# Inverse roots of the rows' variances: on GpSimd by its power operation, in place of VectorE's integer guess and three Newton steps

## What is computed

```python
def _layernorm(x, axis=-1, eps=1e-05):
    m = jnp.mean(x, axis=axis, keepdims=True)
    v = jnp.var(x, axis=axis, keepdims=True)
    return (x - m) / jnp.sqrt(v + eps)
...
    x = L0_attn_x
    xn = _layernorm(x, axis=-1)
    x = x + _L0_attn_ref(xn, ...) + _L0_ffn_ref(xn, ...)
    xn = _layernorm(x, axis=-1)
    x = x + _L1_attn_ref(xn, ...) + _L1_ffn_ref(xn, ...)
```

## Time and profile before

| | |
|---|---|
| time, median of 3 runs | 1029.79 us (1029.18 to 1029.96) |
| the profiled execution's own time | 1030.44 us |
| its span, first to last instruction | 1028.6 us |
| PE busy | 987.3 us (96%) |
| DVE busy | 837.6 us (81%) |
| POOL busy | 767.6 us (75%) |
| ACT busy | 757.0 us (74%) |

### The profile page before, as it was taken

How to read it: one execution, slowest core, us unless ns; L and a number is a source line. 1 busy time by engine, 2 the same in 40 slices (tenths; PEclk the granted TensorE clock), 3 DMA queues, 4 the chain that set the end, 5 groups by cost and what they waited for, 6 DMA issues and landing times.

```text
span 1028.6 us, 23734 instructions
## 1 busy us (share of the span) xinstructions
PE 987.3 (96%) x8004; PEld 678.5 (66%) x8004; DVE 837.6 (81%) x2271; ACT 757.0 (74%) x2014; POOL 767.6 (75%) x942
## 2 busy tenths in 40 slices
PE   5889989999999999999999999999999998999997
PEld 4556655766666666666666666666666665777776
DVE  7989988788878888887778877778778756998875
ACT  5989987567676677676667667676766766999994
POOL 4777668877878787878687778787877545878874
PEclk9999999999999999999999999999999999999999
DMA  8734535234333333343333333333333100000101
GB/s 273 240 110 129 153 103 163 82 120 124 113 106 93 114 93 93 94 119 100 102 93 118 108 95 94 113 94 92 99 103 98 32 1 1 22 22 22 42 22 42
DMA packets 99704, 98.71 MB, mean 96 GB/s; under 512 B 13312, under 2 KB 95360, under 8 KB 98944
## 3 DMA queue, kind: packets, MB, share of 16 engines
q1 hardware_dynamic: 99584, 97.19, 31.0%
HBM read 56.25 MB, written 40.90 MB: 94 GB/s over the span
## 4 chain that ended last, share of the span: by engine, by line
PE 69%; DVE 15%; ACT 7%; issue 4%; POOL 3%; DMA 2%; SPq 0%; DVEq 0%; ACTq 0%; POOLq 0%
PE bank L1650 22%; PE bank L1747 12%; PE bank L1733 12%; PE bank L1764 7%; PE bank L1721 6%; PE bank L1722 5%; DVE arena L1361 2%; PE bank L1943 2%; ACT arena L872 2%; DVE arena L1520 2%; PE bank L1885 2%; POOL arena L628 2%; DVE arena L1377 1%; DMA arena<-in_weights 1%; DVE x_sb L1542 1%
## 5 line engine op out<-in xcount | busy, mean ns | idle before, releaser
L628 POOL TENSOR_SCALAR arena<-arena,rc 128x128 f32<-128x128 f32 (+3 forms) x512 | 277.7, 560 | 178.8 <-DVE rc L1370 177.9
L872 ACT ACTIVATE arena<-arena,nm 128x256 f32<-128x256 f32 (+3 forms) x512 | 283.5, 554 | 112.0 <-DVE nm L1361 107.5
L1361 DVE CUSTOM_DVE_ANT_0 arena<-bank,mask_rows 128x256 f32<-128x256 f32 (+3 forms) x512 | 232.8, 483 | 88.0 <-PE bank L1722 82.9
L1733 PE MATMUL bank<-ident,arena 128*128 128x128 f32 x1280 | 212.0, 278 | 12.4 <-DVE arena L1377 5.1
L1733 PEld LDWEIGHTS bank<-ident,arena 128*128 128x128 f32 x1280 | 149.8, 141 | 72.2 <-DVE arena L1377 29.8
L1722 PE MATMUL bank<-arena 128*128 128x256 f16 (+3 forms) x512 | 152.9, 299 | 0.0
L1747 PE MATMUL bank<-arena 128*64 128x512 f32 (+3 forms) x1024 | 152.0, 439 | 0.0
L1721 PE MATMUL bank<-arena 128*128 128x256 f16 (+3 forms) x512 | 139.9, 300 | 1.7 <-DMA arena<-scr 1.7
L1747 PEld LDWEIGHTS bank<-arena 128*64 128x64 f32 x1024 | 67.8, 136 | 94.8 <-issue 69.8
L1377 DVE COPY arena<-bank 128x512 f32<-128x512 f32 (+3 forms) x256 | 124.4, 486 | 3.7 <-PE bank L1733 3.3
L880 ACT ACTIVATE arena<-bank 128x512 f32<-128x512 f32 (+3 forms) x256 | 108.3, 423 | 15.1 <-PE bank L1733 14.4
(11 more groups left out here) (183 smaller groups left out, 2200.7 us busy)
## 6 DMA issues: line engine op xcount, KB each, us to landing
arena<-scr SPq DMA_DIRECT2D x320, 128.0 KB, 2.7
scr<-arena SPq DMA_DIRECT2D x256, 128.0 KB, 1.7
arena<-in_weights SPq DMA_DIRECT2D x5, 1024.0 KB, 7.7
x_sb<-in_x SPq DMA_DIRECT2D x8, 512.0 KB, 9.1
out<-x_sb SPq DMA_DIRECT2D x16, 256.0 KB, 2.2
xscr<-arena SPq DMA_DIRECT2D x12, 256.0 KB, 3.1
xsh<-xscr SPq DMA_DIRECT2D x6, 256.0 KB, 3.4
xsl<-xscr SPq DMA_DIRECT2D x6, 256.0 KB, 3.7
```

The lines of the kernel that those rows point to most:

```text
L628: last = pool.tensor_scalar(pr[slot][:, OFF[i]:OFF[i + 1]], pr[slot][:, OFF[i]:OFF[i + 1]], rc[:, slot, i:i + 1], 1.0, ALU.mult, ALU.mult)
L872: act.activation(pr[slot][:, OFF[i]:OFF[i + 1]], pr[slot][:, OFF[i]:OFF[i + 1]], ACT.Exp, scale=-1.0, bias=nm[:, slot, i:i + 1], accum_out ...
L1361: dve.tensor_tensor_reduce(pr[slot][:, OFF[i]:OFF[i + 1]], s_tile[i], mask_rows[:, SQ - P * (i + 1):SQ], -1.0, -MASKED, ALU.add, ALU.min, ...
L1733: last = pe.transpose(banks[5 + h][:, (i - j) * P:(i - j + 1) * P], pr[2 * par + h][:, OFF[i] + j * P:OFF[i] + (j + 1) * P], ident[:])
```

## The change

All four sets move from DVE to POOL, and with another method. POOL adds epsilon, raises the sum to the power -0.5 (against a tile `halves_neg` that is filled with -0.5 once), and makes one Newton step in four instructions. With minus the mean and the bias a set has eight instructions; six of them wait on semaphore `root_step` for the one before. On DVE nothing stands in the old places. A set is no longer spread: all its instructions stand together in POOL's list.

```diff
+            pool.memset(halves_neg[:], -0.5).then_inc(consts, 1)
+            pool.wait_ge(consts, 7)
+            ROOT_STEPS = 7
+
+            def inverse_roots(tiles, turn):
+
+                base = ROOT_STEPS * turn
+                mean, var = mv3[:, tiles, 0], mv3[:, tiles, 1]
+                y, t1, t2 = (nw3[:, i, tiles] for i in range(3))
+                pool.tensor_scalar(nbx[:, tiles], mean, -1.0, 1.0, ALU.mult, ALU.mult).then_inc(root_step, 1)
+                pool.tensor_scalar(t1, var, EPS, 1.0, ALU.add, ALU.mult).then_inc(root_step, 1)
+                pool.wait_ge(root_step, base + 2)
+                pool.tensor_tensor(y, t1, halves_neg[:, tiles], ALU.pow).then_inc(root_step, 1)
+                pool.wait_ge(root_step, base + 3)
+                pool.tensor_tensor(t2, y, t1, ALU.mult).then_inc(root_step, 1)
+                pool.wait_ge(root_step, base + 4)
+                pool.tensor_tensor(t2, t2, y, ALU.mult).then_inc(root_step, 1)
+                pool.wait_ge(root_step, base + 5)
+                pool.tensor_scalar(t2, t2, -0.5, 1.5, ALU.mult, ALU.add).then_inc(root_step, 1)
+                pool.wait_ge(root_step, base + 6)
+                pool.tensor_tensor(y, y, t2, ALU.mult).then_inc(root_step, 1)
+                pool.wait_ge(root_step, base + 7)
+                pool.tensor_tensor(nbx[:, tiles], nbx[:, tiles], y, ALU.mult).then_inc(roots_done, 1)
+
+            pool.wait_ge(st3_step, STAT_STEPS)
+            inverse_roots(slice(0, NT), 0)
...
                 normalise(n, 1, n % 2)
+                if n == 0:
+                    pool.wait_ge(act_stats, NB - 3)
+                    pool.wait_ge(st3_step, STAT_STEPS * 3)
+                    inverse_roots(slice(NT, NB * NT), 1)
+                elif n == NR - 5:
+                    pool.wait_ge(st3_step, STAT_STEPS * (NB + 1))
+                    inverse_roots(slice(0, (NB - 2) * NT), 2)
                 rotate(n + AHEAD - 1)
...
             for n in range(-1, NB):
                 body3(n, n % 2)
+                if n == 1:
+                    pool.wait_ge(st3_step, STAT_STEPS * (NB + 3))
+                    inverse_roots(slice((NB - 2) * NT, NB * NT), 3)
...
             row_sums(0)
-            inverse_roots(slice(0, 1), 0)
...
-                if n == NR - 2:
-                    roots_bias(slice(0, (NB - 2) * NT))
-                elif n == -AHEAD:
+                if n == -AHEAD:
...
-                elif NR - 6 <= n <= NR - 3:
-                    roots(slice(0, (NB - 2) * NT), 2, (n - (NR - 6),))
```

More of the change, by code:

```diff
@@ L217, in build @@
         nm3 = sb("nm3", [P, 2, NT], f32)
+        halves_neg = sb("halves_neg", [P, NB * NT], f32)
         x_loaded = [sem(f"x_loaded{b}") for b in range(NB)]
@@ L231, in build @@
         consts = sem("consts")
-        d1 = sem("d1")
+        root_step = sem("root_step")
         roots_done = sem("roots_done")
@@ L424, in build @@
         S_BANK = {1: 1, 0: 2, 2: 2, 3: 3}
+        STAT_STEPS = 2 * NT
         def made(per, n, k=0):
@@ L1073, in link @@
                 dve.wait_ge(s, steps[0])
[L1076 to L1097, removed]
             def statistics(tile, turn):
@@ L1108, in statistics @@
                 dve.wait_ge(st3_step, base + STAT_STEPS)
[L1110 to L1120, removed]
             def normal_rows(b, out, done, count):
@@ L1133, in row_sums @@
                 statistics(b * NT, b)
[L1135 to L1146, removed]
             def row_maximum(b):
@@ L1257, in first_gap @@
             def first_gap(n):
-                if n == 0:
-                    roots(later_tiles, 1, (1, 2), wo)
-                elif n == NB - 1:
+                if n == NB - 1:
                     row_maximum(n)
@@ L1273, in second_gap @@
                     weights_low(G_V, (wv_hi, 1), wv_lo)
-                elif n == 0:
-                    roots(later_tiles, 1, (3,), wo)
-                    roots_bias(later_tiles)
                 elif n == 6:
@@ L1454, in ring @@
                 odd_terms(n + AHEAD)
-                if n == -1:
-                    dve.wait_ge(act_stats, NB - 3)
-                    roots(later_tiles, 1, (0,), wo)
                 inverse(n + 1, 1, e)
@@ L1585, in _ @@
             residual(NB - 1, 1, pj)
-            last_two = slice((NB - 2) * NT, NB * NT)
             for n in range(-1, NB):
@@ L1590, in _ @@
                     row_statistics(NB - 1 + n)
-                elif n < 3:
-                    roots(last_two, 3, (2 * n - 2, 2 * n - 1))
-                if n == 2:
-                    roots_bias(last_two)
         @block.tensor
```

## The result

The changed kernel takes 1045.02 us (median of 4 runs, 1044.37 to 1045.63), the kernel before 1029.88 us beside it. The ratio is 1.0144, with a 95% interval of 1.0128 to 1.0159, so it is slower, by 15.1 us by the medians and by 13.2 to 16.4 us by the interval. The forecast was 1037.3 with a range of 1032 to 1047: the sign and the range held, the size did not. The loss is twice the 7.5 us of the sum.

A forecast was written before the change was run, and what follows sets the result against it. PE was taken as busiest (96%, 69% of the chain), with GpSimd, ScalarE and PE without slack in ring 0. +3.75 - 0.64 + 3.55 - 0.55 + 1.4 = +7.5 us on the 1029.79 median gave 1037.3 us, range 1032 to 1047.

The forecast's parts named there:

- so the whole set goes onto the chain: Ring 0, GpSimd's 28-column set before `rotate(4)`: no slack there, so its full length is added, +3.75 us.
- The power's extra e: Power's cost beyond a plain product, in each set: 1.0 us at 28 columns, 0.85 at 24, 0.3 at 8, 0.15 at 4.
- The short steps: A GpSimd set's eight instructions, power counted as a plain product: 2.75 us for 28 columns, 2.44 for 8.
- Rival C: All GpSimd sets: short instructions at some 0.12 us a step, a set 1.0 us, 1030.6 us, no change; chance 0.10.
- with e five times as large, 1045.9: Upper case of the sum: the power's extra cost in all sets five times the estimate, giving 1045.9 us.
- Start: 4-column set at the kernel's start: ScalarE's normalising begins some 0.4 us later, 1.8 us are free, cost nothing.
- Ring 58: VectorE's first part of the roots is removed in ring 58, ending PE's idle time for a copy: gain 0.64 us.
- Ring 62: VectorE's bias no longer holds ScalarE's normalising in ring 62, and PE's idle time behind it goes: gain 0.55 us.
- Last stage: 8-column set at the end of `body3(1)` delays `key_low(2)`, wanted by PE: 3.1 us less 1.73 cover, cost 1.4 us.
- A: Rival, all sets: a slow power, ten times the estimated extra cost, giving 1056.7 us; chance 0.12.
- B: Rival: power code must be loaded, 1.28 us before each of the three later sets, giving 1041.1 us; chance 0.06.
- D: Rival, behind the start: VectorE is the bound, its 39 lost instructions are worth 9.0 us, giving 1020.8 us; chance 0.04.

The follow-up runs named there:

- the run with the product: The changed kernel with a product in place of the power in all four sets, so the roots are not computed: 1038.7 us, ratio 1.0080.
- the pair again: Second run of the kernel before with sets 2 and 3 on GpSimd, in ring 60 and `body3(2)`: 1028.05 us, ratio 0.9977.

## Why the forecast held in sign and not in size

- **What bounds, and which edits cost:** right. The two sets in front of `rotate` carry the loss (8.5 and 8.3 us, of which gains elsewhere give some back), and moving one of them past the last `rotate` took away all it cost. The step "so the whole set goes onto the chain" held: of 6.97 us in ring 0, 6.6 came through, and of 6.29 in ring 59, 6.4 by the landmarks.
- **The power's extra e: mis-sized, by 4.6.** The step that failed is "some 17 passes, so e = 1.0 us at 28 columns". A product of that shape takes 0.24 us, the power 4.82, so e was 4.6 us; 3.9 against 0.85 at 24 columns, 1.4 against 0.3 at 8, and 0.83 against 0.15 at 4. The forecast's rule that it grows with the columns was right, but the estimate rested on no row. With the measured sets (6.97 and 6.29 in place of 3.75 and 3.55) the sum would have been +13.5 us, or 1043.3.
- **The short steps:** near enough. Seven of them took 2.15 us where the forecast had 2.75 less 0.25 for the power's plain product, 2.5. (For 8 columns its own rows make some 2.5 us instead of 2.44.) The steps were 0.28 to 0.33 us apart. Rival C's 0.12 us a step is out. So is the estimate of 3.2 us a set by a factor of two between the engines: at 8 columns GpSimd's short steps took 0.20 to 0.21 us, all but the first, and VectorE's in the kernel before mostly 0.17.
- **The clock: not in the forecast.** I took a wait's price to be its length. Two waits of about 7 us cost 3.7 us together on top, shown by the run that kept PE busy. With them the 13.5 us become 17.2, where the landmarks without the stretches that vary make 16.3 and the medians 15.1. Most of the 1.2 us between those two is the kernel before: 34 of its 53 executions beside the experiments had a mean granted clock under 0.999, and their median is 1.3 us above that of the others, while three of the four executions of the changed kernel had 0.993, which is what its two long stretches make alone. As an estimate that is 1.3 x 34/53 = 0.8 us by which the kernel before is usually slower than these landmarks have it. The stated case "with e five times as large, 1045.9" came within 1 us of the result, but not by a complete account: it had the power nearly right and had no clock in it. That the range held the result is luck to that extent.
- **Start:** right. ScalarE began at 9.31 instead of 8.72, 0.6 later where 0.4 was said, and set 0 alone makes no difference.
- **Ring 58:** right, -0.7 against -0.64, and the run with set 2 alone keeps it. **Ring 62:** right in kind: ScalarE's normalising at 847.96 has no wait before it where it had 0.98; 0.86 us came back instead of 0.55.
- **Last stage:** +1.1 against +1.4, by errors that cancel. The set took 4.04 us instead of 3.1: the power took 1.65 where the forecast had 0.5, and the first instruction 0.63, at a time when VectorE's pair of mixes ran. By the landmarks only 1.35 us of that came through, where 4.04 less the cover of 1.73 makes 2.3. PE waited 1.56 us for `key_low` at 934.60, as said. Behind that 0.25 came back.
- **The rivals:** A was the right direction, at 4.6 times e instead of ten. B fell: the first power, 1.03 us, lies on the line of all the others. The Trainium skill's 6 us for a first call (GPSIMD Engine Reference, section 2.1) did not show up in this case: that power took 1.03 us. D fell as well: VectorE lost 12.0 us of work, and 1.5 us of that were gained, in rings 58 and 62.

## What to carry to other kernels

Before an operation is moved onto an engine that others wait for, find what stands behind it in that engine's order. The same eight instructions cost 8.3 us in front of the last `rotate` and nothing one ring later, and only with the set there did the kernel become faster than before. An operation that the trace of before does not show deserves to be measured by its shape before the rest of a sum is refined. A wait of several us in front of PE should be priced with the slower matmuls behind it, and a repeating stage should be compared by the length of one round.

## What the runs showed of the hardware

- GpSimd's elementwise power of two tiles takes 0.40 us + 0.158 us a column, on 16 partitions as on 128, with exponents -0.5 and 2 alike; a product of the same 28 columns takes 0.24.
- TensorE was granted 0.50 of its clock after standing still for 7.25 and 6.65 us, for about 4 us of work in each ring, and behind 7.24 us in the run with set 1 alone. Behind short waits it came and went: not behind 2.57 us in ring 0 of the run with the product, but behind 2.69 us at the same place (granted 0.54 to 0.61 over 4 us) of the run with the power in the last set only. At the turn to the last stage, behind a wait of 1.65 us in the kernel before, it was slowed in five of the thirteen profiles, kernels with the same order of work there among both kinds. In four profiles (the product, PE kept busy, set 3 alone, the pair again) a short stretch at 0.50 came near 47 or 55 us, behind waits of 3.19, 2.23, 1.97 and 2.08 us, but none came behind 2.92 us at that place in the profile of set 2 alone.
- The last stage has two steady patterns, of 20.57 and 21.77 us a batch. In both, VectorE's pair of two-input operations from SBUF overlaps GpSimd's subtraction of 1024 columns. In the fast one the pair takes 1.95 us and the subtraction 2.56, in the slow one 3.56 and 2.13. 1.4 us more on GpSimd in set 3 moved the kernel from the slow pattern to the fast one.
